# Low-rank products of the gate and up projections: one matmul per product, or four 32-row matmuls per pair of hidden tiles

## The reference

```
def _qlora_linear(x, wq, A, B):
    w = jnp.tile(wq, (1, 4))
    base = x @ w.T
    lora = x @ A.T @ B.T
    return base + lora * 0.5
gate = silu(_qlora_linear(x, w1q, a1, b1))
up = _qlora_linear(x, w3q, a3, b3)
return _qlora_linear(gate * up, w2q, a2, b2)
```

## Time and profile before

| what | us |
|---|---|
| median of three runs | 635.8 |
| the profiled execution, its own time | 637.71 |
| span of the profiled execution | 635.9 |
| granted TensorE clock over the span, share of full | 0.989 |
| TensorE (PE) busy | 602.4 |
| VectorE (DVE) busy | 518.8 |
| ScalarE (ACT) busy | 418.8 |
| GpSimd (POOL) busy | 136.9 |

### The profile page before, as it was taken

How to read it: one execution, slowest core, us unless ns; L and a number is a source line. 1 busy time by engine, 2 the same in 40 slices (tenths; PEclk the granted TensorE clock), 3 DMA queues, 4 the chain that set the end, 5 groups by cost and what they waited for, 6 DMA issues and landing times.

```text
span 635.9 us, 12441 instructions
## 1 busy us (share of the span) xinstructions
PE 602.4 (95%) x3432; PEld 446.4 (70%) x3432; DVE 518.8 (82%) x1299; ACT 418.8 (66%) x1165; POOL 136.9 (22%) x140
## 2 busy tenths in 40 slices
PE   4778999999999999999999999999999999889996
PEld 4676767776677677776777777767678888665664
DVE  5887788888888888888888888888877988889456
ACT  4455678777778777777877777868873545265343
POOL 2122122212221232122221322123000000025620
PEclk9898999999999999999999999999999999999999
DMA  8000201202112022021120210203283000001003
GB/s 314 30 1 1 83 17 69 82 0 82 37 45 82 0 82 67 15 82 37 45 82 0 82 54 28 82 19 134 84 272 147 2 1 0 31 0 51 0 18 115
DMA packets 13862, 37.80 MB, mean 59 GB/s; under 512 B 1328, under 2 KB 1584, under 8 KB 13584
## 3 DMA queue, kind: packets, MB, share of 16 engines
q1 hardware_dynamic: 13840, 37.53, 17.4%
HBM read 31.24 MB, written 6.29 MB: 59 GB/s over the span
## 4 chain that ended last, share of the span: by engine, by line
PE 78%; DVE 12%; issue 4%; ACT 3%; DMA 1%; POOL 0%; ACTq 0%; DVEq 0%; SPq 0%; POOLq 0%
PE bank L996 13%; PE bank L1037 13%; PE bank L998 13%; PE bank L997 13%; PE bank L1049 13%; PE bank L1067 3%; PE bank L1059 2%; DVE dot L848 2%; PE bank L1006 2%; PE bank L1020 2%; PE bank L1019 2%; DVE ss L651 1%; PE bank L1213 1%; ACT pr L375 1%; DVE st L822 1%
## 5 line engine op out<-in xcount | busy, mean ns | idle before, releaser
L375 ACT ACTIVATE pr<-ss,small 128x128 f32<-128x128 f32 (+3 forms) x256 | 143.2, 559 | 38.9 <-DVE small L651 38.4
L383 ACT ACTIVATE pt<-bank 128x128 f32<-128x128 f32 (+3 forms) x256 | 110.7, 432 | 62.4 <-PE bank L1037 62.3
L651 DVE CUSTOM_DVE_ANT_0 ss<-bank,cst 128x128 f32<-128x128 f32 (+3 forms) x256 | 123.4, 486 | 15.9 <-PE bank L998 10.3
L1037 PEld LDWEIGHTS bank<-ident,pr 128*128 128x128 f32 x640 | 75.5, 142 | 66.6 <-ACT pr L375 34.0
L1037 PE MATMUL bank<-ident,pr 128*128 128x128 f32 x640 | 118.9, 284 | 3.1 <-ACT pr L375 3.0
L290 POOL TENSOR_TENSOR qrot<-qrot,qswp 64x512 f32<-64x512 f32 x64 | 82.1, 1283 | 103.4 <-DVE qrot L637 103.3
L996 PE MATMUL bank<-kt_hi,qt_hi 128*128 128x128 f32 (+3 forms) x256 | 100.8, 394 | 3.3 <-DVE qt_lo L641 2.4
L1049 PE MATMUL bank<-pt,kvn 128*64 128x256 f32 (+3 forms) x512 | 86.1, 448 | 0.7 <-ACT pt L383 0.7
L998 PE MATMUL bank<-kt_hi,qt_lo 128*128 128x128 f32 (+3 forms) x256 | 83.2, 325 | 0.0
L997 PE MATMUL bank<-kt_lo,qt_hi 128*128 128x128 f32 (+3 forms) x256 | 82.9, 324 | 0.0
L641 DVE TENSOR_TENSOR qt_lo<-qrot,qt_hi 128x512 fp32r<-128x512 f32 x64 | 60.1, 939 | 24.5 <-ACT qt_hi L365 24.3
(11 more groups left out here) (168 smaller groups left out, 1135.1 us busy)
## 6 DMA issues: line engine op xcount, KB each, us to landing
sv<-sv SPq DMA_DIRECT2D x16, 576.0 KB, 3.7
sq<-sq SPq DMA_DIRECT2D x16, 448.0 KB, 3.4
wvo_scratch<-vs SPq DMA_DIRECT2D x16, 256.0 KB, 2.0
wv_raw<-wvo_scratch SPq DMA_DIRECT2D x8, 512.0 KB, 4.2
xa<-x SPq DMA_DIRECT2D x8, 256.0 KB, 5.6
x<-x SPq DMA_DIRECT2D x1, 2048.0 KB, 11.0
out<-yo SPq DMA_DIRECT2D x8, 256.0 KB, 2.0
w<-w SPq DMA_DIRECT2D x1, 1376.0 KB, 13.3
```

Source lines behind the costliest of these rows:

```text
L375: nc.scalar.activation(pr[:, k % 4, 0:n], ss[:, k % 2, 0:n], ACT.Exp, bias=negmax[:, k % 8:k % 8 + 1], scale=-1.0, accum_out=rsum[:, k:k + ...
L383: nc.scalar.activation(pt[:, b, h, 0:i + 1, i * P:(i + 1) * P], bank[2 + k % 2][:, 0:(i + 1) * P].rearrange("p (j q) -> p j q", q=P), ACT. ...
L651: nc.vector.tensor_tensor_reduce(out=ss[:, k % 2, 0:n], in0=bank[k % 2][:, 0:n], in1=mask[:, SEQ - n:SEQ], scale=-SCALE, scalar=3.4e38, op ...
L1037: last = nc.tensor.transpose(bank[2 + k % 2][:, j * P:(j + 1) * P], pr[:, k % 4, j * P:(j + 1) * P], ident[:, :])
```

## The change

The low-rank product leaves `gate_or_up`. After each odd tile a new function `low_rank` runs four matmuls of 32 rows, at rows 0, 32, 64 and 96 of the array: gate and up of the even tile, gate and up of the odd tile. Each adds to its own bank and increments `gate_made` or `up_made`. The operands have a new layout: one `lx` of 128 rows in place of `lg` and `lu`, `bs` and `bs_s` of 128 rows, and in each block of 32 rows the three partial products (hi by hi, and the two with a lo part) lie in six rows. ScalarE writes `lx` with one operation and VectorE completes it with one; the copies into `lt` become two.

```diff
-    lg = pro.take("lg", [P, TOK], F32R)
-    lu = pro.take("lu", [P, TOK], F32R)
+    lx = pro.take("lx", [P, TOK], F32R)
-    lt = pro.take("lt", [P, 2, 96])
+    lt = pro.take("lt", [P, 2, 4, 32])
+    dt = pro.take("dt", [P, 2, 2 * RANK])
...
-    bs = nc.alloc_sbuf_tensor_at("bs", [96, HID], F32, offset=start + 4 * P + 32)
+    bs = nc.alloc_sbuf_tensor_at("bs", [P, HID], F32, offset=start + 4 * P + 32)
...
-    bs_s = ffn.take("bs_s", [96, HID], F32R)
+    bs_s = ffn.take("bs_s", [P, HID], F32R)
...
             def lora_hi(u):
                 act.wait_ge(c.y_turned, u + 1)
-                nc.scalar.activation(lg[0:96, u * P:(u + 1) * P], bank[4][0:96, 0:P], ACT.Copy,
-                                     scale=cst[0:96, 3 * SEQ:3 * SEQ + 1])
-                nc.scalar.activation(lu[0:96, u * P:(u + 1) * P], bank[4][0:96, 0:P], ACT.Copy,
-                                     scale=cst[0:96, 3 * SEQ + 1:3 * SEQ + 2]).then_inc(c.lp_hi_made, 1)
+                nc.scalar.activation(lx[:, u * P:(u + 1) * P], bank[4][:, 0:P], ACT.Copy,
+                                     scale=cst[:, 3 * SEQ:3 * SEQ + 1]).then_inc(c.lp_hi_made, 1)
...
-                for k, l in enumerate((lg, lu)):
-                    last = nc.vector.scalar_tensor_tensor(l[64:96, u * P:(u + 1) * P], bank[4][64:96, 0:P],
-                                                          cst[64:96, 3 * SEQ + k:3 * SEQ + k + 1],
-                                                          l[64:96, u * P:(u + 1) * P].bitcast(F32),
-                                                          ALU.mult, ALU.subtract)
-                last.then_inc(c.lp_split, 1)
+                nc.vector.scalar_tensor_tensor(lx[:, u * P:(u + 1) * P], bank[4][:, 0:P], cst[:, 3 * SEQ + 1:3 * SEQ + 2],
+                                               lx[:, u * P:(u + 1) * P].bitcast(F32), ALU.mult, ALU.add)\
+                  .then_inc(c.lp_split, 1)
...
-                    nc.vector.tensor_copy(lt[:, u % 2, 32:96].rearrange("p (g n) -> p g n", n=32)[:, :, 0:2 * RANK],
-                                          lt[:, u % 2, 0:2 * RANK].unsqueeze(1).to_broadcast([P, 2, 2 * RANK]))\
-                      .then_inc(c.dots_made, 1)
+                    for j in (0, 2):
+                        last = nc.vector.tensor_copy(
+                            lt[:, u % 2, j:j + 2, 0:6].rearrange("p w (c n) -> p w c n", c=3),
+                            dt[:, u % 2, :].rearrange("p (w n) -> p w n", w=2).unsqueeze(2).to_broadcast([P, 2, 3, RANK]))
+                    last.then_inc(c.dots_made, 1)
...
-                    nc.vector.tensor_tensor(bs_s[32:64, :], bs[32:64, :], bs_s[32:64, :].bitcast(F32), ALU.subtract)\
-                      .then_inc(g.bs_split, 1)
+                    nc.vector.scalar_tensor_tensor(bs_s[:, :], bs[:, :], cst[:, 3 * SEQ + 6:3 * SEQ + 7], bs_s[:, :].bitcast(F32),
+                                                   ALU.mult, ALU.add).then_inc(g.bs_split, 1)
...
-            def gate_or_up(which, G, n, hf):
-                r, k = n // FOLD, n % FOLD
-                rows, j, tok = RROWS[r], k * W2C + r * P, slice(hf * SEQ, (hf + 1) * SEQ)
-                out = bank[(GATE, UP)[which][G % 3]][0:rows, :]
-                three(out, w13_hi[:, which, j:j + rows], w13_lo[:, which, j:j + rows], xf_hi[:, tok], xf_lo[:, tok],
-                      True, False)
-                return nc.tensor.matmul(out, bs_s[:, j:j + rows], (lg, lu)[which][0:96, tok], start=False, stop=True)
+            def hidden(which, G):
+
+                n, tok = G % 12, slice(G // 12 * SEQ, (G // 12 + 1) * SEQ)
+                j = n % FOLD * W2C + n // FOLD * P
+                return bank[(GATE, UP)[which][G % 3]][0:RROWS[n // FOLD], :], slice(j, j + RROWS[n // FOLD]), tok
+
+            def gate_or_up(which, G):
+                out, cols, tok = hidden(which, G)
+                three(out, w13_hi[:, which, cols], w13_lo[:, which, cols], xf_hi[:, tok], xf_lo[:, tok], True, False)
+
+            def low_rank(G):
+
+                for j in range(4):
+                    out, cols, tok = hidden(j % 2, G + j // 2)
+                    nc.tensor.matmul(out, bs_s[32 * j:32 * j + 32, cols], lx[32 * j:32 * j + 32, tok], start=False, stop=True,
+                                     tile_position=(32 * j, 0)).then_inc((g.gate_made, g.up_made)[j % 2], 1)
...
-                    gate_or_up(0, G, n, hf).then_inc(g.gate_made, 1)
+                    gate_or_up(0, G)
                     if G >= 3:
                         pe.wait_ge(g.gu_made, G - 2)
-                    gate_or_up(1, G, n, hf).then_inc(g.up_made, 1)
+                    gate_or_up(1, G)
+                    if G % 2:
+                        low_rank(G - 1)
```

More of the change, by code:

```diff
@@ L554, in _ @@
                     act.wait_ge(c.bs_in, 16)
-                    nc.scalar.activation(bs_s[:, :], bs[:, :], ACT.Copy).then_inc(g.bs_hi_made, 1)
+                    nc.scalar.activation(bs_s[:, :], bs[:, :], ACT.Copy, scale=cst[:, 3 * SEQ + 5:3 * SEQ + 6]).then_inc(g.bs_hi_made, 1)
                     act.wait_ge(c.xt2_moved, QB)
@@ L848, in lora_dots @@
                     nc.vector.tensor_tensor_reduce(out=dot[:, j % 2, :], in0=xn2[:, :], in1=a13[:, j, :], scale=1.0, scalar=0.0,
-                                                   op0=ALU.mult, op1=ALU.add, accum_out=lt[:, u % 2, j:j + 1])\
+                                                   op0=ALU.mult, op1=ALU.add, accum_out=dt[:, u % 2, j:j + 1])\
                       .then_inc(c.dots_raw, 1)
@@ L867, in _ @@
             split_output(1, 0)
-            nc.vector.memset(lt[:, :, :], 0.0).then_inc(c.lt_zero, 1)
+            nc.vector.memset(lt[:, :, :, :], 0.0).then_inc(c.lt_zero, 1)
             for t in range(TB + 1):
@@ L1191, in turn_y @@
                 nc.tensor.transpose(bank[4][:, P:2 * P], fold[:, u % 2, :], ident[:, :])
-                nc.tensor.transpose(bank[4][0:96, 0:P], lt[:, u % 2, :], ident[:, :]).then_inc(c.y_turned, 1)
+                nc.tensor.transpose(bank[4][:, 0:P], lt[:, u % 2, :, :].rearrange("p g n -> p (g n)"), ident[:, :]).then_inc(c.y_turned, 1)
             pe.wait_ge(a.r_moved, 2 * PAIRS - 1)
@@ L1304 @@
     cst[96:128, 2 * SEQ:3 * SEQ] = -sin.T
-    for g in range(3):
-        cst[32 * g:32 * g + 2, 3 * SEQ] = LORA_SCALE
+    for g in range(4):
+        cst[32 * g:32 * g + 6, 3 * SEQ] = np.array([1, 1, -1, -1, 1, 1]) * LORA_SCALE
         cst[32 * g + 2:32 * g + 4, 3 * SEQ + 1] = LORA_SCALE
+        cst[32 * g:32 * g + 6, 3 * SEQ + 5] = [1, 1, 1, 1, -1, -1]
+        cst[32 * g + 4:32 * g + 6, 3 * SEQ + 6] = 1
     for k in range(FOLD):
@@ L1327 @@
     w13 = np.stack([I["ffn_w1q"].T, I["ffn_w3q"].T], 1)
-    bs = put((96, HID), *[(slice(32 * g + 2 * k, 32 * g + 2 * k + 2), I[n].T)
-                          for g in range(3) for k, n in enumerate(("ffn_b1", "ffn_b3"))])
+    bs = put((P, HID), *[(slice(32 * g + 2 * k, 32 * g + 2 * k + 2), I[("ffn_b1", "ffn_b3")[g % 2]].T)
+                         for g in range(4) for k in range(3)])
     a13 = np.broadcast_to(np.concatenate([I["ffn_a1"], I["ffn_a3"]]), (P, 2 * RANK, D))
```

## The result

The changed kernel takes 632.04 us (median of 15 runs, 629.75 to 635.44) against 636.13 for the kernel before (15 runs beside them, 634.35 to 637.72): a ratio of 0.9932, 95% interval 0.9915 to 0.9950. That is 4.1 us less by the medians, where 2.3 was forecast; the interval allows 3.2 to 5.4. The profiled execution's span is 629.1 us instead of 635.9.

A forecast was written before the change was run, and what follows sets the result against it. TensorE was taken to bound the hidden layer's second half, VectorE the first. Start of tile 12 -0.6, second half -2.6 and stall +0.9 sum to -2.3 us: from 635.8 to 633.5 us, range 631.3 to 636.3 (8 in 10).

The forecast's parts named there:

- cheap group: Rival, 20%: in the hidden layer shape changes cost little and four row-group matmuls cost 0.31 us; 631.9 us in all.
- Price of a group: Hidden layer, TensorE: four 32-row matmuls in row groups cost 0.55 us together, between 0.30 and 1.2.
- merged changes of shape: Second half of the hidden layer: three down products directly behind a row group save 0.1 us each, -0.3 together.
- Second half: Hidden layer from tile 12, bound by TensorE: six pairs save -2.3 us, with merged shape changes -2.6.
- No overlap: Rival, 9%: the array serves the row groups one after the other, a group costs 1.2 us; slower, 637.2 us.
- loads in line: Rival, 18%: matmuls overlap but the four loads go one by one at 0.11 us, group 0.9; 635.2 us.
- Stall at token tile 3: Down projection: TensorE waits for `z` behind GpSimd's two sums in line, 0.4 to 1.2 us, taken as +0.9.
- Projection stage: Ahead of the hidden layer: VectorE loses a 0.27 us correction per token tile and gains a copy; start -0.4 us.
- `bs` operation: Projection stage, VectorE: this 1.58 us operation now takes a scalar and is put at 0.1 us more.
- First half: Hidden layer up to tile 12, set by VectorE's chain: tile 12 starts -0.6 us, with tile 0 0.4 earlier.
- `gu` of tile 8: First half, VectorE: it must wait for the pair 8, 9 on TensorE and so comes 0.9 us later.
- saved matmuls give nothing directly: First half: no direct gain from fewer matmuls, since TensorE waits for weight splits behind `gu` on VectorE.

The follow-up runs named there:

- tile0_first: Changed kernel with statistics and normalisation of token tile 0 ahead of the last `fs_hi`, `fs_lo` and `l2` in ScalarE's and VectorE's order: 631.49 us.
- layout_tokens: The kernel of tokens_early with a full-array low-rank matmul again behind each gate and each up, as in layout_only: 632.99 us.
- tokens_early: Changed kernel with the preparation of the second half's tokens on ScalarE and VectorE moved from hidden tile 9 to tile 7: 630.49 us.
- layout_only: Changed kernel with its new operand layout, but a full-array low-rank matmul (128 rows) behind each gate and each up: 632.85 us.

## Why the prediction was right or wrong

The direction, the size of the two terms that I worked out most closely, and the range were right. The median moved by 4.1 us where the sum said 2.3; the shortfall is in two terms. The time by itself would have named the wrong mechanism: 632.04 us lies outside the forecast's own band (632.8 to 634.4) and next to the rival "cheap group" (631.9), whose cheap group the trace doesn't show.

- **Price of a group: 0.62 us, 0.55 forecast.** Entry and exit cost what the column groups had shown, plus longer loads. The merged changes of shape saved 0.15 each, not 0.1. Second half -2.67 against -2.6. Six groups net of the merging come to 0.51 us each: 23.34 less 72 steps of 0.234 and three down products of 1.15.
- **"No overlap" fell** with the four matmuls in 0.50 us, **"loads in line"** with the four loads in 0.19. **"Cheap group" fell** on its premise: the group costs twice the 0.31 us. That figure was an estimate from the 3.07 times of the Trainium skill ("TensorE: Matmul & The Clock Gate", section "Measured speedup vs the span model"); against the 0.93 us of four matmuls in line the measured gain is 1.5 times. The trace fits the Trainium skill ("TensorEngine Tiling (Array Packing)", section "Key Properties"), by which changing the tiling mode drains the array: the gap into the group is 0.32 us instead of 0.23, and that out of the first full matmul behind it 0.34.
- **Stall at token tile 3: 0.90 us, +0.9 forecast.** It came by the route and at the place given, and moving token tile 0 ahead removed it.
- **Projection stage, "one correction of 0.27 us per token tile": mis-sized, -0.4 against -1.44.** I took the distance between the two corrections as the price of one and left out the gaps around them, though the earlier trace rows show them: the second correction begins at 541.77 and the next operation at 542.14, 0.37 later, for a 0.34 us operation. An operation on 128 partitions of that length lets the next begin after 0.26. The saving is 0.63 per token tile, less 0.08 for the second copy. The `bs` operation, forecast 0.1 dearer, became 0.06 cheaper (1.56 us to the next start, 1.62 before); it had run on rows 32 to 64 and now runs on all 128.
- **First half, -0.2 against -1.35.** The same term again (about 1.1 us for two token tiles), and `gu` of tile 8 came 1.06 us later relative to tile 0, where I had 0.9: VectorE waited 1.46 us for it. Then the profiled execution had a short `xf_lo`, 0.68 us, where I had kept 1.24. With a long one (tile0_first) the first half takes 28.97, -0.2 as forecast, but that is luck: VectorE's saving was larger than I had it, and `xf_lo` took 1.64 us instead of 1.24. The second half may then lose 1.6 more to the clock. Up to tile 12 both kernels have the same order, so the changed kernel's other runs can meet either; how the median mixes them isn't known, and 4.1 and the profile's 4.5 don't differ beyond the interval. I hadn't named this hazard: TensorE's wait ahead of tile 12 was 0.75 us before and can be 1.69 now, after which the clock fell.
- **Two causes, by runs.** With the tokens moved, the row groups and their new order are worth 2.5 us net (layout_tokens against tokens_early): 0.97 in the first half and 2.48 in the second, less 0.93 for the stall. So "saved matmuls give nothing directly" in the first half holds only as long as TensorE waits for `xf_lo` at its end. The layout's part is 1.43 us ahead of tile 0 and, in the first half, 0.43 as measured in layout_only.

## What to carry to other kernels

Small low-rank products with at most 32 rows can share the array, but each visit costs one change of shape in and out, here 0.62 - 0.23 = 0.4 us: put such groups next to each other, and count what comes late because their results are held back to the end of a pair. Price an operation that goes by the starts around it, not by its neighbours of the same kind. Measure a change of a few microseconds from a fixed point behind the stages that it doesn't touch. And look for two engines that meet by a tenth of a microsecond: which of `xf_lo` and the sum came first decided over 0.68 or 1.6 us, and with the tokens, splits and token tile 0 all moved the kernel took 627.8 us instead of 632.0.

## What was unexpected of the hardware

- A VectorE correction on partitions 64 to 96 among operations that start at partition 0 came with three gaps of 0.12 us: ahead of it, behind it, and ahead of the next one that reads PSUM. An operation on 88 partitions from 0 had none.
- `xf_lo` and GpSimd's sum hold each other up whole: 0.68 or 1.6 us for the same VectorE operation, beside starts 0.10 and 0.17 us behind the sum's. That so small a difference decides it was read from the 14 profiles, not set by an experiment.
- After waits of 1.69 and 1.76 us TensorE went on at 1.2 GHz for over 3 us (a matmul each 0.43 us), which cost 1.6 us; after four of 1.59 to 1.62 it didn't.
- The start of the kernel, up to the same operation, took 461.75 to 465.47 us in 14 profiles; between 27 and 70 us the granted clock was 0.92 in the earliest and 0.84 in the latest.
- Four loads of 32 rows and 128 columns, in four row groups, took 0.19 us together, as long as one full load.
